# A CIN tower on one core: GpSimd adds sixteen product slots of a tile, VectorE's closing sums go, and layer 1 runs in full fp32

## The reference

```python
cur1 = relu(einsum('bpd,pn->bnd', (e[:, :, None] * e[:, None]).reshape(b, 32 * 32, d), filter_0))
cur2 = relu(einsum('bpd,pn->bnd', (e[:, :, None] * cur1[:, None]).reshape(b, 32 * 128, d), filter_1))
z = sum over d of concatenate([cur1, cur2], axis=1)          # 512 x 256
h = relu(concatenate([z, dense_ctx]) @ W_top1 + b_top1)      # 512
h = relu(h @ W_top2 + b_top2)                                # 256
y = h @ W_top3
```

## Time and profile before

| | |
|---|---|
| median of three runs | 989.07 us |
| profiled execution, its own time | 989.63 us |
| its span, from the first to the last instruction | 987.70 us |
| granted clock of TensorE, mean | 0.997 of 2.4 GHz |
| VectorE busy | 949.2 us, 96% |
| TensorE busy | 873.7 us, 88% |
| GpSimd busy | 873.8 us, 88% |
| ScalarE busy | 693.7 us, 70% |

### The profile page before, as it was taken

The page is one execution under the profiler, slowest core; times in us unless marked ns, Lnnn a source line. Parts: engine busy times, 40 slices in busy tenths (PEclk is TensorE's granted clock), DMA queues, the critical chain, the costliest instruction groups (busy, mean ns, idle before and its releaser), DMA issues.

```text
span 987.7 us, 18157 instructions
## 1 busy us (share of the span) xinstructions
PE 873.7 (88%) x3581; PEld 667.3 (68%) x3581; DVE 949.2 (96%) x2422; ACT 693.7 (70%) x2230; POOL 873.8 (88%) x739
## 2 busy tenths in 40 slices
PE   3999888989888899888898988898988898988998
PEld 2667666767666677666676766676766666766774
DVE  3799999999999999999999999999999999999993
ACT  2677767777777777777776776776777777777772
POOL 5499999999999999999999999999999999998970
PEclk9999999999999999999999999999999999999998
DMA  6821122222122222122222112222212222202000
GB/s 178 219 77 49 38 72 76 76 77 60 29 67 76 76 77 70 33 54 74 77 76 76 46 39 71 76 76 76 59 29 69 76 76 77 69 26 58 1 0 1
DMA packets 37336, 65.10 MB, mean 66 GB/s; under 512 B 6084, under 2 KB 17316, under 8 KB 37317
## 3 DMA queue, kind: packets, MB, share of 16 engines
q1 hardware_dynamic: 31538, 59.99, 21.5%
q0 software_dynamic: 4096, 2.11, 1.4%
q10 hardware_dynamic: 1683, 2.80, 0.9%
HBM read 60.67 MB, written 4.20 MB: 66 GB/s over the span
## 4 chain that ended last, share of the span: by engine, by line
DVE 57%; issue 23%; PE 14%; DVEq 3%; DMA 2%; SPq 1%; POOL 0%; ACT 0%
DVE part L558 26%; DVE z_lo L511 10%; DVE z L499 6%; DVE whole L574 5%; DVE part L553 4%; DVE z_last L503 3%; PE t_dve L752 3%; PE t_dve L754 2%; PE t_dve L753 2%; PE t_act L752 2%; PE t_act L754 2%; PE t_act L753 2%; DVEq L557 2%; DVE weigh L485 1%; DMA x_rows<-emb 1%
## 5 line engine op out<-in xcount | busy, mean ns | idle before, releaser
L405 ACT ACTIVATE prod<-t_act,weigh 128x128 f32<-128x128 f32 x2048 | 585.0, 369 | 145.9 <-PE t_act L754 141.7
L287 POOL TENSOR_TENSOR prod<-prod 128x896 f32<-128x896 f32 x381 | 564.1, 1481 | 24.2 <-ACT prod L405 2.8
L558 DVE SCALAR_TENSOR_TENSOR part<-t_dve,weigh,part 128x128 f32<-128x128 f32 x1792 | 473.0, 334 | 0.1
L752 PE MATMUL t_dve<-w_hi,cur_hi 128*128 128x512 f32 x512 | 207.0, 404 | 93.2 <-DVE part L558 93.2
L752 PE MATMUL t_act<-w_hi,cur_hi 128*128 128x512 f32 x512 | 212.8, 416 | 0.1
L754 PE MATMUL t_act<-w_hi,cur_lo 128*128 128x512 f32 x512 | 200.1, 391 | 0.0
L754 PE MATMUL t_dve<-w_hi,cur_lo 128*128 128x512 f32 x512 | 200.0, 391 | 0.0
L753 PE MATMUL t_act<-w_lo,cur_hi 128*128 128x512 f32 x512 | 199.8, 390 | 0.0
L753 PE MATMUL t_dve<-w_lo,cur_hi 128*128 128x512 f32 x512 | 199.7, 390 | 0.0
L752 PEld LDWEIGHTS t_dve<-w_hi,cur_hi 128*128 128x128 f32 x512 | 96.0, 187 | 141.6 <-DVE part L558 121.7
L257 POOL DMA_INDIRECT emb<-table_dram,row_ids x128 | 131.6, 1028 | 26.2 <-issue 18.4
(11 more groups left out here) (87 smaller groups left out, 680.7 us busy)
## 6 DMA issues: line engine op xcount, KB each, us to landing
x_shift<-x_rows SPq DMA_DIRECT2D x64, 512.0 KB, 5.9
x_pair<-x_rows SPq DMA_DIRECT2D x96, 128.0 KB, 4.5
x_same<-x_rows SPq DMA_DIRECT2D x32, 256.0 KB, 3.0
x_rows<-emb SPq DMA_DIRECT2D x64, 64.0 KB
w_raw<-w_dram ACTq DMA_DIRECT2D x8, 256.0 KB, 4.4
emb<-table_dram,row_ids POOLq DMA_INDIRECT x128, 2.4
w_raw<-wt_dram SPq DMA_DIRECT2D x2, 512.0 KB, 5.3
v<-w0a_dram ACTq DMA_DIRECT2D x1, 256.0 KB
```

The costliest lines, as they stand in the source:

```text
L287: nc.gpsimd.tensor_tensor(src[:, dst, :], src[:, dst, :], src[:, other, :], ALU.add).then_inc(folded, 1)
L405: last = nc.scalar.activation(prod[i][:, HEADS * k + j, :], t_act[k % ARING][:, j * MAPS:(j + 1) * MAPS], ACT.Copy, scale=weigh[p][:, i, h ...
L558: nc.vector.scalar_tensor_tensor(dst, src, w, dst, ALU.mult, ALU.add).then_inc(added, 1)
L752: nc.tensor.matmul(bank[:, :], cur_hi[p][:, cols], w_hi[:, w], start=True, stop=False)
```

## The change

- Layer 1: groups 2 and 3 are no longer split. All four groups are fp32 matmuls (line 716), and v_hi, v_lo, z_hi, z_lo, round_pair and both lower_pair functions go.
- VectorE's running sums stay in slots 0 and 1 of prod[i], where they began; part and whole go.
- GpSimd folds all sixteen slots: 8, 4 and 2 slots, then the last addition to side[p], which is now the whole sum of the tile. A fold waits for ScalarE's sixteen slots and for VectorE's sixteen additions.
- finish and last_side go. VectorE does the last tile's folds and last addition itself (last_fold).
- relu2 and lower2 read side[p]. relu2 moves behind tile 2 on ScalarE, lower2 to just before tile 3 on VectorE, pooling behind tile 3 on TensorE, products 0 to between tiles 0 and 1, products 2 to between tiles 1 and 2.
- The perceptron's pool1 halves, which shared z_hi and z_lo, get tensors of their own.

The diff, cut to what the prediction speaks of:

```diff
-FOLDS = [(slice(2, 9), slice(9, 16)), (slice(2, 5), slice(5, 8)), (slice(2, 4), slice(4, 9, 4))]
+HALVE = (slice(0, 8), slice(8, 16))
+FOLDS = [HALVE, (slice(0, 4), slice(4, 8)), (slice(0, 2), slice(2, 4))]
...
-        z_hi = sb("z_hi", [128, SPLIT, COLS], f32r)
-        z_lo = sb("z_lo", [128, SPLIT, COLS], f32r)
...
-        part = [sb(f"part{p}", [128, TILES, 2, MAPS]) for p in range(2)]
         prod = [sb(f"prod{i}", [128, FEEDS, MAPS]) for i in range(TILES)]
         side = [sb(f"side{p}", [128, TILES, MAPS]) for p in range(2)]
-        whole = sb("whole", [128, TILES, MAPS])
-        v_b = whole
+        v_b = side[0]
...
-            def lower_pair(c, p):
-                pool.wait_ge(pair_rounded, c)
-                pool.wait_ge(layer1_done, c)
-                nc.gpsimd.tensor_tensor(z_lo[:, 0, :], z[p][:, WHOLE, :], z_hi[:, 0, :].bitcast(fp32),
-                                        ALU.subtract).then_inc(z_parts_ready, 1)
             def fold(c, i, p, staged=None):
                 src = prod[i]
                 tile = c * TILES + i
+                done = tile * len(FOLDS)
                 pool.wait_ge(weighed, (tile + 1) * HALF)
+                pool.wait_ge(added, (tile + 1) * FEEDS)
                 for step, (dst, other) in enumerate(FOLDS):
                     if step > 0:
-                        pool.wait_ge(folded, tile * len(FOLDS) + step)
+                        pool.wait_ge(folded, done + step)
                     nc.gpsimd.tensor_tensor(src[:, dst, :], src[:, dst, :], src[:, other, :], ALU.add).then_inc(folded, 1)
-                pool.wait_ge(folded, (tile + 1) * len(FOLDS))
+                pool.wait_ge(folded, done + len(FOLDS))
                 if i == 0:
-                    wait(pool, summed, (c - 1) * 2)
+                    wait(pool, cur2_ready, c - 1)
                 if staged is not None:
                     pool.wait_ge(row_ids_ready, staged + 1)
-                nc.gpsimd.tensor_tensor(side[p][:, i, :], src[:, 2, :], src[:, 3, :], ALU.add).then_inc(side_ready, 1)
+                nc.gpsimd.tensor_tensor(side[p][:, i, :], src[:, 0, :], src[:, 1, :], ALU.add).then_inc(side_ready, 1)
...
-            def round_pair(c, p):
-                act.wait_ge(z_ready, c * 3 + 3)
-                act.wait_ge(layer1_done, c)
-                nc.scalar.activation(z_hi[:, :, :], z[p][:, WHOLE:GROUPS, :], ACT.Copy).then_inc(pair_rounded, 1)
             def relu2(c, p):
-                act.wait_ge(summed, c * 2 + 2)
+                act.wait_ge(side_ready, (c + 1) * TILES)
                 wait(act, pool2_done, c - 1)
-                nc.scalar.activation(cur2_hi[p][:, :, :], whole[:, :, :], ACT.Relu).then_inc(cur2_hi_ready, 1)
+                nc.scalar.activation(cur2_hi[p][:, :, :], side[p][:, :, :], ACT.Relu).then_inc(cur2_hi_ready, 1)
             def weigh_tile(c, i, p):
                 tile = c * TILES + i
                 wait(act, side_ready, tile - TILES + 1)
-                wait(act, added, (tile - TILES) * FEEDS + 2)
...
-                    if i == 0 and not (isinstance(c, int) and c + 1 >= CHUNKS):
-                        round_pair(c + 1, 1 - p)
...
-                    if i == 1 and not (isinstance(c, int) and c == 0):
+                    if i == 2 and not (isinstance(c, int) and c == 0):
                         relu2(c - 1, 1 - p)
...
-            def lower_pair(c, p):
-                dve.wait_ge(pair_rounded, c)
-                dve.wait_ge(layer1_done, c)
-                nc.vector.tensor_tensor(z_lo[:, 1, :], z[p][:, WHOLE + 1, :], z_hi[:, 1, :].bitcast(fp32),
-                                        ALU.subtract).then_inc(z_lo_ready, 1)
...
-                    wait(dve, summed, (c - 1) * 2)
...
-                        dst = part[p][:, i, step % 2, :]
+                        dst = prod[i][:, step % 2, :]
                         w = weigh[p][:, i, h:h + 1]
                         if step < 2:
                             if step == 0:
                                 dve.wait_ge(weighed, tile * HALF + 1)
-                            nc.vector.scalar_tensor_tensor(dst, src, w, prod[i][:, step, :],
-                                                           ALU.mult, ALU.add).then_inc(added, 1)
+                            nc.vector.scalar_tensor_tensor(dst, src, w, dst, ALU.mult, ALU.add).then_inc(added, 1)
                         else:
                             dve.wait_ge(added, tile * FEEDS + step - 1)
                             nc.vector.scalar_tensor_tensor(dst, src, w, dst, ALU.mult, ALU.add).then_inc(added, 1)
-            def last_side(p):
+            def last_fold(p):
+                src = prod[TILES - 1]
                 dve.wait_ge(weighed, CHUNKS * TILES * HALF)
-                nc.vector.tensor_reduce(side[p][:, TILES - 1, :], prod[TILES - 1][:, 2:FEEDS, :].rearrange("x h n -> x n h"),
-                                        AX.X, ALU.add).then_inc(last_side_ready, 1)
-            def finish(c, p):
-                dve.wait_ge(added, (c + 1) * (TILES * FEEDS))
-                wait(dve, cur2_hi_ready, c)
-                wait(dve, cur2_ready, c)
-                nc.vector.tensor_tensor(whole[:, :, :], part[p][:, :, 0, :], part[p][:, :, 1, :], ALU.add).then_inc(summed, 1)
-                if isinstance(c, int) and c == CHUNKS - 1:
-                    dve.wait_ge(side_ready, CHUNKS * TILES - 1)
-                    last_side(p)
-                    dve.wait_ge(last_side_ready, 1)
-                else:
-                    dve.wait_ge(side_ready, (c + 1) * TILES)
-                dve.wait_ge(summed, c * 2 + 1)
-                nc.vector.tensor_tensor(whole[:, :, :], whole[:, :, :], side[p][:, :, :], ALU.add).then_inc(summed, 1)
+                dve.wait_ge(added, CHUNKS * TILES * FEEDS)
+                for step, wide in enumerate((8, 4, 2)):
+                    if step > 0:
+                        dve.wait_ge(last_folded, step)
+                    nc.vector.tensor_tensor(src[:, 0:wide, :], src[:, 0:wide, :], src[:, wide:2 * wide, :],
+                                            ALU.add).then_inc(last_folded, 1)
+                dve.wait_ge(last_folded, 3)
+                nc.vector.tensor_tensor(side[p][:, TILES - 1, :], src[:, 0, :], src[:, 1, :], ALU.add).then_inc(side_ready, 1)
...
-                dve.wait_ge(summed, c * 2 + 2)
                 dve.wait_ge(cur2_hi_ready, c + 1)
                 wait(dve, pool2_done, c - 1)
-                nc.vector.scalar_tensor_tensor(cur2_lo[p][:, :, :], whole[:, :, :], 0.0,
+                nc.vector.scalar_tensor_tensor(cur2_lo[p][:, :, :], side[p][:, :, :], 0.0,
...
                 add_tile(c, 0, p)
-                if more1:
-                    lower_pair(c + 1, 1 - p)
-                if not (fixed and c == 0):
-                    finish(c - 1, 1 - p)
-                add_tile(c, 1, p)
-                if not (fixed and c == 0):
-                    lower2(c - 1, 1 - p)
                 if more2:
                     products(c + 2, p, 0)
+                add_tile(c, 1, p)
+                if more2:
                     products(c + 2, p, 2)
                 add_tile(c, 2, p)
                 if more1:
                     lower(c + 1, 1 - p)
                     pooling1(c + 1, 1 - p)
                 place(c, p)
+                if not (fixed and c == 0):
+                    lower2(c - 1, 1 - p)
                 add_tile(c, 3, p)
...
-            finish(CHUNKS - 1, (CHUNKS - 1) % 2)
+            last_fold((CHUNKS - 1) % 2)
...
                 for g in groups:
-                    if g < WHOLE:
+                    if g < GROUPS:
                         if g == 0:
                             pe.wait_ge(z_ready, c * 3 + 1)
+                        elif g == WHOLE:
+                            pe.wait_ge(z_ready, c * 3 + 3)
                         nc.tensor.matmul(acc1[:, :], v[:, g, :], z[p][:, g, :], start=g == 0, stop=False)
-                    elif g < GROUPS:
-                        k = g - WHOLE
-                        if k == 0:
-                            pe.wait_ge(z_parts_ready, c * 2)
-                        else:
-                            pe.wait_ge(z_lo_ready, c)
-                        nc.tensor.matmul(acc1[:, :], v_hi[:, k, :], z_hi[:, k, :], start=False, stop=False)
-                        nc.tensor.matmul(acc1[:, :], v_lo[:, k, :], z_hi[:, k, :], start=False, stop=False)
-                        nc.tensor.matmul(acc1[:, :], v_hi[:, k, :], z_lo[:, k, :], start=False, stop=False)
                     else:
+                        pe.wait_ge(z_parts_ready, c)
...
                 layer2(c, 2, p)
+                layer2(c, 3, p)
                 if not (fixed and c == 0):
                     pooling(c - 1, 1 - p)
-                layer2(c, 3, p)
```

More of the change, by code:

```diff
@@ L69, in dlrm_tower @@
         v_last = sb("v_last", [3 * FIELDS, MAPS])
-        v_hi = sb("v_hi", [128, SPLIT, MAPS], f32r)
-        v_lo = sb("v_lo", [128, SPLIT, MAPS], f32r)
```

(15 more changed lines are left out.)

## The result

The change makes the kernel slower: 1069.86 us, the median of four runs (1067.69 to 1070.68), against 990.06 us for the kernel before in the same comparison (988.86 to 992.97). The ratio is 1.0798, 95% interval [1.0767, 1.0829]. Forecast were 984.4 us and, at most, 998.

What follows compares the result with a forecast made beforehand. GpSimd's full queue was taken as the bound, steady at 29.34 us a chunk against 29.35. Start, steady chunks and end summed to 2.4 + 0 - 1.7 - 5.4 = -4.7 us on 989.07, giving 984.4; range 960 to 998.

Steps and rivals of the forecast that it cites:

- part 4: Moved products 0, lower2, relu2 and pooling: no instruction or DMA added; 5 us of lead covers lower2's wait.
- Part 3: GpSimd adding sixteen slots: 2.21 us more a chunk; its wait for VectorE's additions costs nothing in steady state.
- Rival 6: GpSimd's folds wait for VectorE's additions at today's phases: 2.58 us idle a chunk, 72 us, 1056; chance 0.08.
- The sum along GpSimd's queue: GpSimd's steady chunk: 29.35 - 1.24 - 0.98 + 2.21 = 29.34 us, so no change.
- rival 5: Turns with VectorE's five remaining two-input operations cost GpSimd more: 0.5 us a chunk, 14 us, 998; chance 0.15.
- open gaps forecast on VectorE: Sign of being right: VectorE idle at times, with some 24 us of work a chunk.
- the start: Chunk 0 on GpSimd: first fold waits for tile 0's additions, so chunk 1 starts 2.4 us later.
- the end: Chunk 29 and the last seven tiles on GpSimd through ScalarE's last relu2: 1.7 and 5.4 us back.
- Rival 4: VectorE was the bound after all: chunk falls to 26.5 us, 78 us less, 906; chance 0.05.
- Rival 3: GpSimd blocked throughout each removed VectorE operation: 2.07 us returned instead of 0.98, 31 us, 954; chance 0.05.
- Rival 2: VectorE's products meet GpSimd's gathers instead of folds, hardly disturbing each other: 0.87 us a chunk, 24 us, 960; chance 0.22.

Runs made afterwards that it cites:

- run 1: The changed kernel with only products 0 put back behind tile 1: 991.8 us, ratio 1.0001 to the kernel before.
- run 2: The changed kernel with the gathers a tile earlier on GpSimd, products 0 left where the change put them: 999.54 us, ratio 1.0085.
- run 8: The changed kernel with the last gather of a chunk a tile later, behind tile 3: 1233.17 us, a single run.
- run 4: The kernel before with only products 0 moved up, to before tile 1: 1020.14 us, ratio 1.0293.
- run 7: The kernel before with the slots changed and relu2, lower2 and pooling moved; layer 1 still split, products 0 behind tile 1: 1039.05 us, ratio 1.0488.
- run 6: The changed kernel with products 0 back behind tile 1 and the gathers a tile earlier: 991.98 us, ratio 1.0015.
- run 5: The changed kernel with GpSimd folding only slots 2 to 15, without waiting for VectorE's additions, whose sums are mostly left out of the result: 935.15 us, ratio 0.9459.
- run 3: The kernel before with only layer 1 in full fp32: 942.37 us, ratio 0.9503.
- run 9: On run 3, VectorE keeps four running sums instead of two and GpSimd folds twelve slots: 915.11 us, ratio 0.9237 to the kernel before.
- run 12: The kernel before with products 0 before tile 1 and the gathers a tile earlier: 989.99 us, ratio 1.0012.

## Why the prediction was wrong

**The step that failed** stands in part 4: "Products 0 moves a tile earlier ... They add no instruction and no DMA". The move adds none, but products 0 begin with a wait, for the x_shift transfer, and I never asked when that lands. The trace of before had it (SyncE's timeline; the page's DMA issues, KB and us to landing; VectorE's timeline):

```profile
505.21 0.61 SPq L218 DMA_DIRECT2D x_shift<-x_rows  x1
```

```profile
x_shift<-x_rows SPq DMA_DIRECT2D x64, 512.0 KB, 5.9
```

```profile
518.39 1.76 DVE L499 TENSOR_TENSOR z<-x_shift,x_same 128x1024 f32<-128x1024 f32 x1
```

Requested at 505.21, with 5.9 us to landing, the transfer is there at about 511.1; products 0 start at 518.39, 7.3 us later. The move takes tile 1's additions away from ahead of them (4.1 us), the change takes lower2 (1.1 us), line 511 and the two closing sums (5.7 us together) away too. Products 0 would be asked for at 507.4, right behind tile 0, and be 3.7 us early on the very first turn. Runs 1, 2 and 8 each move only this balance, by -78, -70 and +163 us from the changed kernel. In run 4, where line 511 and the closing sums still stand ahead of products 0, the transfer is in time; what that run loses is something else (see there).

**Part 3** failed with it: the wait for the additions was costed at nothing, because "Each tile is ready about 5 us early". With the products in their old place that was right: in run 7 the additions end 3 to 10 us before the folds for most tiles (the folds wait 7.5 us in all), in run 6 4.6 us or more in every one. In the changed kernel tile 1's end 0.1 us before its fold can start, which had stood idle for some 3 us. Run 5 shows that the wait is what lets the late transfer reach GpSimd. I had named the gathers queued behind this wait and didn't follow them further, to the transfer and back to VectorE.

**Rival 6** named the right symptom, folds waiting for VectorE, and a time of 1056 near the measured 1070. Its reason was another, the phases of the kernel before: 2.58 us idle a chunk. Run 7, with the wait but not the early products, shows that these cost next to nothing. That the measured chunk is 2.62 us longer is luck. The rival had 0.08 and wasn't in the range.

**The sum along GpSimd's queue held.** With the loop removed (run 6) GpSimd takes 29.6 us a chunk, forecast 29.34. What the last quarter of a microsecond consists of I didn't resolve; it lies in the direction of rival 5. (Run 1 gives 29.5, but still has waits of the loop in it.) The open gaps forecast on VectorE don't show in run 6. It is busy 94% of the span instead of some 24 us a chunk, with the 1024-column products at 2.95 and 3.99 us (533.51 and 544.85) beside GpSimd's folds. In run 6 chunks 1 to 27 cost 6.9 us instead of nothing, the start 4.3 instead of 2.4, and the end gives 9.0 back instead of 7.1: +2.2 us where the sum said -4.7. So even without the loop the change would have been no gain (ratios 1.0001 and 1.0015 in runs 1 and 6).

**The parts.** Layer 1 in fp32 alone gives -49 us (run 3), the slots alone +49 (run 7), both with products 0 behind tile 1 nothing (run 1), and the moved products +78. Measured for the whole were +80.

**Rival 4**, VectorE as the bound, is refuted: run 7 takes 2.6 us a chunk from VectorE and the kernel gets slower by 49 us; run 9 gives VectorE work over run 3, and it gets faster by 27. **Rival 3**, GpSimd blocked for the whole of a VectorE operation, needed 28.2 us a chunk; run 6 gives 29.6. Run 3 takes line 274 and one such operation out and GpSimd's chunk shortens by 29.36 - 27.90 = 1.46 us, where 1.24 + 0.33 was summed and 1.24 + 0.69 would be the full length. The rows of before show why. The 384-column fold began at 510.16, when only 0.47 us of z_lo were left (to 510.63), and took 0.33 us longer. The rule of the Trainium skill (SBUF — State Buffer, "SBUF: two separate sides") is that the other engine is fully blocked. It prices this turn at no more than these 0.47 us; the 0.69 was the prediction's own reading of it. The trace stays a little below the rule. **Rival 2**'s reason was wrong: a gather that begins beside a 1024-column product takes 1.79 us (runs 4 and 12), so these do take turns. Its gather at the start ran beside operations of 0.69 us.

**TensorE's clock** fell in every run with gaps on TensorE: 0.93 in the changed kernel, 0.874 in run 8, 0.954 in run 7, 0.997 before. In the changed kernel it is a consequence: the turns of the loop contain no matmul, and at the one place where slow matmuls could reach GpSimd, the fold of tile 2, the slots are ready 1.5 us or more before it. (TensorE's 26% of the chain on the page come from stretches in which the chain was followed another way back.) Whether a part of the loss in the runs at 0.95 to 0.98 is due to the clock, I didn't separate.

## What to carry to other kernels

When an operation is moved, list what it waits for as well as what it issues, transfers above all, and take the slack from the trace: the time from landing to use. Shorten that by everything that the rest of the change takes away ahead of it. Then look for a closed path: here the new wait joined GpSimd's folds to a transfer that its own gathers start, and from then on the length of this path set the pace, 12.3 us of transfers and 19.6 us of work in series, and no engine's own queue. Where two engines are both without idle time and take turns at memory, sum each queue for itself, without the waits, before believing either's busy time.

## What was not expected of the hardware

A gather beside a 1024-column VectorE product with two SBUF inputs took 1.79 us instead of 0.97, also at 529.29 in the changed kernel (1.73). In all 28 such places of run 4 it ends 0.86 us after the product does, so it passes almost wholly behind it. VectorE's cast of 128 columns (line 549) took 2.85 us at 573.62 in the changed kernel, and ended 0.1 us after GpSimd's 1024-column fold; in most chunks it takes 0.21. An operation with one SBUF input waits for GpSimd's folds as well at times. GpSimd's additions kept to the line through 128 and 896 columns closely: 2.41 us for 1024 against 2.40.
